# A conditioned sequence model on one Trainium2 core: the second layer as one stage

## The reference, cut to what matters

```python
xn = layernorm(x, norm_scale, norm_bias)
q, k, v = xn @ Wq + bq, xn @ Wk + bk, xn @ Wv + bv
k = where(mask, -inf, k);  v = where(mask, 0.0, v)
q = softmax(q over the 32 features of a head)
k = softmax(k over the 1024 rows of a batch)
attn = einsum('bhse,bhsd->bhed', k, v)          # 32 x 32 for each head
y = einsum('bhtd,bhed->bhte', q, attn)
h = silu(layernorm(y) * (1 + scale(emb)) + shift(emb))
out = x + h @ film_out_W + film_out_b
```

## Time and profile before

| | us |
|---|---|
| device time, median of 3 runs | 6635.8 (6633.12 to 6639.58) |
| span of the profiled execution | 6635.1 |
| p2, from its first ScalarE table load to the first load of the next stage | 1722.7 to 2093.4: 370.7 |
| linear_attention | 2093.4 to 2326.5: 233.1 |
| p3, to the first table load of ssm_inputs | 2326.5 to 2492.95: 166.5 |

### The profile page before, as it was taken

How to read it: one execution, slowest core, us unless ns; L and a number is a source line. 1 busy time by engine, 2 the same in 40 slices (tenths; PEclk the granted TensorE clock), 3 DMA queues, 4 the chain that set the end, 5 groups by cost and what they waited for, 6 DMA issues and landing times. The chain is left out here.

```text
span 6635.1 us, 86376 instructions
## 1 busy us (share of the span) xinstructions
PE 5586.8 (84%) x30592; PEld 3543.3 (53%) x30592; DVE 4664.3 (70%) x5664; ACT 4230.4 (64%) x6243; POOL 2482.7 (37%) x1098
## 2 busy tenths in 40 slices
PE   6999999997897578999578888887999578888884
PEld 2446666664443543444466666663444366666662
DVE  2329999995322544554799999994554599999993
ACT  1218888884111424554798998982555599999992
POOL 0000000000000000000599999991000299999995
PEclk9999999998998789999799999999999799999997
DMA  5344424323323343333555565552333555655554
GB/s 202 146 134 95 96 65 100 76 56 115 138 99 117 138 165 121 142 144 148 164 152 156 160 161 158 157 141 104 142 143 130 163 160 155 158 152 154 154 151 171
DMA packets 598091, 909.84 MB, mean 137 GB/s; under 512 B 104473, under 2 KB 243865, under 8 KB 597157
## 3 DMA queue, kind: packets, MB, share of 16 engines
q1 hardware_dynamic: 586212, 879.10, 44.4%
q0 software_dynamic: 5120, 16.78, 0.7%
q10 hardware_dynamic: 6336, 8.52, 0.4%
HBM read 577.82 MB, written 326.39 MB: 136 GB/s over the span
## 5 line engine op out<-in xcount | busy, mean ns | idle before, releaser
L1624 POOL TENSOR_TENSOR scan_hC<-scan_h,scan_Crep 128x1024 f32<-128x1024 f32 x1024 | 2395.0, 2371 | 2619.5 <-DVE scan_h L1857 2594.7
L1788 ACT ACTIVATE scan_a<-scan_dt,scan_A 128x512 f32<-128x512 f32 x2048 | 1368.9, 697 | 94.0 <-DVE scan_h L1857 76.7
L1658 PE MATMUL scan_y<-ident,scan_hC 128*128 128x128 f32 x8192 | 1112.0, 279 | 294.8 <-POOL scan_hC L1624 289.9
L1658 PEld LDWEIGHTS scan_y<-ident,scan_hC 128*128 128x128 f32 x8192 | 902.2, 141 | 682.4 <-POOL scan_hC L1624 634.5
L1857 DVE TENSOR_TENSOR_SCAN scan_h<-scan_a,scan_carry,scan_h 128x512 f32<-128x512 f32 x1024 | 1216.8, 1260 | 17.9 <-ACT scan_a L1788 14.9
L1857 DVE TENSOR_TENSOR_SCAN scan_h<-scan_a,scan_h 128x512 f32<-128x512 f32 x1024 | 1155.5, 1200 | 59.2 <-ACT scan_a L1788 58.5
L1764 ACT COPY scan_h<-scan_drive 128x1024 f32<-128x1024 f32 x1024 | 1042.2, 1018 | 164.6 <-PE scan_drive L1646 152.5
L1646 PE MATMUL scan_drive<-scan_Bd,scan_dT 128*128 128x256 f32 x4096 | 749.7, 305 | 130.0 <-ACT scan_h L1764 79.0
L1646 PEld LDWEIGHTS scan_drive<-scan_Bd,scan_dT 128*128 128x128 f32 x4096 | 557.7, 192 | 183.3 <-issue 96.3
L791 DVE CUSTOM_DVE_ANT_0 att_sm<-att_S,att_mneg 128x1024 f32<-128x1024 f32 x512 | 622.1, 1215 | 15.0 <-POOL att_mneg L717 14.8
L849 ACT ACTIVATE att_pr<-att_sm,att_nmax 128x1024 f32<-128x1024 f32 x512 | 590.5, 1153 | 56.3 <-DVE att_nmax L791 44.0
(11 more groups left out here) (162 smaller groups left out, 5967.4 us busy)
## 6 DMA issues: line engine op xcount, KB each, us to landing
scan_dT<-scratch_dtuT SPq DMA_DIRECT2D x512, 256.0 KB, 5.5
scratch_dtuT<-ssmin_dT SPq DMA_DIRECT2D x128, 512.0 KB, 3.5
scan_Crep<-scratch_bc SPq DMA_DIRECT2D x64, 1024.0 KB, 9.1
att_q<-scratch_q_split SPq DMA_DIRECT2D x256, 128.0 KB, 4.3
att_k<-scratch_k_split SPq DMA_DIRECT2D x256, 128.0 KB, 4.5
scratch_uD<-ssmin_uD SPq DMA_DIRECT2D x64, 512.0 KB, 3.4
scratch_z<-ssmin_zt SPq DMA_DIRECT2D x128, 256.0 KB, 2.1
scratch_dt<-ssmin_dt SPq DMA_DIRECT2D x64, 512.0 KB, 2.6
```

Source lines behind the costliest of these rows:

```text
L1624: nc.gpsimd.tensor_tensor(hC[k % 2][:], of, Crep[:, 2 * p:2 * p + 2, :], ALU.mult).then_inc(s["scaled"].handle, 1)
L1658: last = nc.tensor.matmul(y[j][:, t, :], hC[k % 2][:, i, t * P:(t + 1) * P], ident[:], start=(p == 0 and i == 0 and t == 0), stop=False, i ...
L1788: nc.scalar.activation(a[(2 * k + i) % 3][:], dt[j][:], ACT.Exp, scale=A[:, m, 2 * p + i:2 * p + i + 1]).then_inc(s["decayed"].handle, 1)
```

## The change

`project` p2, `linear_attention` and `project` p3 become one stage, `linear_layer`, written out without a loop. k, q, v and y stay in SBUF; only x1 is read (once for the statistics, once as the residual) and x2 written. One TensorE order runs through all batches (`order` in the diff): k of this batch, the transposes ("w") and the products ("o") of the film projection of the batch before, q, v, the transposes of k and q, attn ("a"), the transposes ("x") of the next batch's x, and y. Each entry takes the next of the 8 banks and waits until the entry 8 back has been emptied. x and xT have one buffer each instead of two; y lies in q's buffer; the softmax of q runs in two halves of 2048 columns; y is now copied by VectorE; residual and result have 4 tiles each instead of 8. In `Rows`, arguments were added so that the source of the rows may be tiles already in SBUF (`made`) and xT may have one buffer (`turned=1`).

```diff
-        project(core, "p2", ...)
-        linear_attention(core, ident, io, scr)
-        project(core, "p3", ...)
+        linear_layer(core, ident, eps, io, cols, scr)

+        def order():
+            yield from (("x", 0, k) for k in range(8))
+            for it in range(B):
+                yield from (("k", it, k) for k in range(8))
+                if it:
+                    yield from ((kind, it - 1, k) for kind in ("w", "o") for k in range(8))
+                yield from ((kind, it, k) for kind in ("q", "v", "kt", "qt") for k in range(8))
+                yield "a", it, 0
+                if it + 1 < B:
+                    yield from (("x", it + 1, k) for k in range(8))
+                yield from (("y", it, k) for k in range(8))
+            yield from ((kind, B - 1, k) for kind in ("w", "o") for k in range(8))
...
+            # SyncE, after the first x, the tables, the 4 weights, rows and mask
+            for it in range(B):
+                if it + 1 < B:
+                    xs.load(sp, it + 1)      # waits until x(it) has been transposed
+                    load_mask(it + 1)        # waits until mneg(it) is made
+                if it:
+                    leave(it - 1)            # 4 residual loads ahead, then store a tile, load a tile
+            leave(B - 1)
...
+            # TensorE, for each entry e of order()
+                if e >= 8:
+                    before, of, which = entries[e - 8]
+                    pe.wait_ge(taken[before].handle, taken[before].at(per[before] * of + which + 1))
+            # kt waits for k_norm; qt for q_norm of its half; a for all of kt and v taken;
+            # y for a taken and its half of qt; o for its half of w; k for its half of x
...
+            # ScalarE
+            for it in range(B):
+                for k in range(8):
+                    take_k(it, k)
+                    if k == 1 and it:
+                        ys.root(act, it - 1)
+                    if k == 5:
+                        exp_k(it, 0)
+                exp_k(it, 1)
+                if it:
+                    for k in range(8):
+                        ys.take(act, it - 1, k, *at_bank("w", it - 1, k))
+                exp_k(it, 2)
+                exp_k(it, 3)
+                if it + 1 < B:
+                    xs.root(act, it + 1)
+                for h in range(2):
+                    exp_q(it, h)
+                for t in range(TT):
+                    take_kt(it, t)
+                for k in range(8):
+                    take_qt(it, k)
+                for k in range(8) if it + 1 < B else ():
+                    xs.take(act, it + 1, k, *at_bank("x", it + 1, k))
+            ys.root(act, B - 1)
+            for k in range(8):
+                ys.take(act, B - 1, k, *at_bank("w", B - 1, k))
...
+            # VectorE
+            for it in range(B):
+                make_mneg(it)
+                if it:
+                    stats(ys, it - 1)
+                shift_k(it, 0)
+                if it:
+                    ys.center(dve, it - 1)
+                for m in range(1, KT):
+                    shift_k(it, m)
+                for t in range(TT):
+                    if it:
+                        take_o(it - 1, t)
+                    if it + 1 < B:
+                        xs.take_stats(dve, it + 1, t)
+                    if t == 3:
+                        norm_k(it)
+                if it + 1 < B:
+                    xs.aggregate(dve, it + 1)
+                for t in range(TT):
+                    take_q(it, t)
+                    if t == 1 and it + 1 < B:
+                        xs.center(dve, it + 1)
+                    if t == 3:
+                        shift_q(it, 0)
+                shift_q(it, 1)
+                for t in range(TT):
+                    take_v(it, t)
+                    if t == 1:
+                        norm_q(it, 0)
+                    if t == 3:
+                        norm_q(it, 1)
+                take_a(it)
+                for t in range(TT):
+                    take_y(it, t)
+            stats(ys, B - 1)
+            ys.center(dve, B - 1)
+            for t in range(TT):
+                take_o(B - 1, t)
```

More of the change, by code:

```diff
@@ L404, in stage_added @@
         n = len(self.x)
-        for k in range(2 * n):
+        for k in range(2 * n) if self.made is None else ():
             self.rows_in[k].stage_added(self.per_half * B // n)
@@ new lines, in linear_layer @@
+        row = [sb(f"row{n}", [P, D]) for n in range(3)]
+        kp = sb("keep", [P, B, TT])
+        res, out = ([sb(f"{n}{k}", [P, D]) for k in range(4)] for n in ("res", "out"))
+        banks = [psum(f"bank{k}", [P, HALF]) for k in range(8)]
+        kinds = ("k", "q", "v", "kt", "qt", "a", "y", "o")
+        per = {**{kind: 8 for kind in kinds}, "a": 1, "x": 8, "w": 8}
+        taken = {kind: core.count("lin_taken_" + kind) for kind in kinds}
+        xs = Rows(core, sb, 1, scr["x1"], scr["tab"][2], ACT.Identity, eps, ident, turned=1)
@@ new lines, in linear_layer @@
+        ys = Rows(core, sb, 1, None, scr["tab"][3], ACT.Silu, eps, ident, turned=1, made=(y, taken["y"]))
+        taken["x"], taken["w"] = xs.evacuated, ys.evacuated
+        lin = {n: core.count("lin_" + n) for n in ("mask_in", "k_shift", "k_exp", "k_norm", "q_max", "q_shift", "q_exp",
+                                                   "q_norm", "q_sums", "k_inverse", "mneg", "cleared")}
+        w = lambda eng, n, value: eng.wait_ge(lin[n].handle, lin[n].at(value))
+        full, stored, res_in = core.bank_full, core.stage_stored, core.slot_in
@@ new lines, in linear_layer @@
+        weights_in = [core.count(f"weights_in{n}") for n in range(4)]
+        N_CONST = 16 * 4
+        def order():
[10 more added lines that the diff above has]
+            yield from ((kind, B - 1, k) for kind in ("w", "o") for k in range(8))
@@ new lines, in linear_layer, with await_full @@
+        entries = list(order())
+        place = {entry: e for e, entry in enumerate(entries)}
+        at_bank = lambda *entry: (banks[place[entry] % 8], full[place[entry] % 8], place[entry] // 8 + 1)
+        def await_full(eng, *entry):
+            _, c, uses = at_bank(*entry)
+            eng.wait_ge(c.handle, c.at(uses))
+        qv = lambda h: q[:, 4 * h:4 * h + 4, :].rearrange("p k (g e) -> p (k g) e", e=DH)
+        some = lambda x, h: x[:, 4 * H * h:4 * H * (h + 1)]
+        wide = lambda x, h: some(x, h).unsqueeze(2).broadcast_to([P, 4 * H, DH])
@@ L915, in store_y @@
[L915 to L930, removed]
@@ new lines, in leave @@
+            def leave(it):
+                for t in range(4):
+                    load_res(it, t)
+                for t in range(TT):
+                    store_out(it, t)
+                    if t + 4 < TT:
+                        load_res(it, t + 4)
+            xs.load(sp, 0)
+            xs.load_table(sp)
+            load_weight(0, "Wk")
+            load_mask(0)
+            load_weight(1, "Wq")
+            load_row(0, 2)
+            load_weight(2, "Wv")
+            load_row(1, 3)
```

323 lines of the change are left out of this document (200 added, 123 removed).

## The result

The changed kernel takes 6475.36 us, median of 4 runs (6471.62 to 6479.7), beside 6637.69 for the kernel before in the same comparison: ratio 0.9753, 95% interval 0.9739 to 0.9767. The forecast was 6467 (6452 to 6498). The span of the profiled execution is 6469.7 us, 165.4 less than before. In the table further down two of e8's six executions (6611.58 and 21171.61 us, at a granted clock of 0.92 and 0.52) were disturbed: its median of 6461.37 holds them, that of the other four is 6457.4, its ratio is formed without them, and of the single executions of e4 and e5 it can't be told.

The account below looks back on a forecast made before the run. TensorE bounds p2; in linear_attention no engine does, they wait in turn. Start, products, transposes, attn and y, waits and tail sum to 601.1 us for 770.25, 169.2 less: 6467 us, range 6452 to 6498.

Parts of the forecast that it names:

- One TensorE list that sets the pace: New stage: priced as one TensorE list, TensorE busy over 93% at a clock of 0.97 or more.
- Start, 20.9: Start of the stage: first x load, statistics and 8 transpose groups before products, 20.9 us, as in ssm_inputs.
- Products, 439.5: 128 products in the stage, 32 for each batch, 3.43 us each: 439.5 us.
- Transposes 49.7, attn and y 59.3: TensorE's small work: 14 blocks of 8 transpose groups, 49.7 us; eight attn and y groups of 7.41, 59.3 us.
- w to o, 9.0: Film transposes to film products: TensorE waits 3.0 us for ScalarE's chain, three times, 9.0 us.
- Tail, 21.4: After the last y: uncovered chain 15.1 us, slow-clock product start 2.1, end 4.2; together 21.4 us.
- VectorE, ScalarE, SyncE hidden: Whole stage: these engines' work fits beside TensorE's; VectorE 80 us a batch against TensorE's 142.
- Slack of 1.6 us at the v tiles: Last v tile emptied at 56.4, its bank wanted by a transpose group at 58.0: VectorE may be 1.6 us late.
- rival (2): VectorE late at the v tiles by 5 to 8 us each batch: 20 to 32 us, 6486 to 6498; chance 0.13.
- Rival (1), the clock falls in the small work: Transposes at 1.2 GHz cost 54 us, total 6520; attn and y too, 6580; chance 0.07.
- Rival (3), 745 us without overlap: Interleaving does not overlap anything: four batches of 181 us plus 21, stage 745, total 6611; chance 0.03.
- The stage's sum, 601.1: All terms of the TensorE list added: 601.1 us for the new stage, against 770.25 before.

Follow-up runs that it names:

- e8: Changed kernel with film transposes between the last k products; last batch: y statistics tile by tile during ScalarE's copies, attn between q's transpose halves; stage 581.64 us, median 6461.37.
- e4: Changed kernel with two unused reductions of half of q (4.6 us) on VectorE before the last four v tiles of each batch; stage 600.56 us.
- e5: Changed kernel with four unused reductions of half of q (9.2 us expected) on VectorE before the last four v tiles of each batch; stage 622.67 us.
- e2: Changed kernel without interleaving: each batch in the order of its own dependences, one stage, nothing through DRAM; stage 717.35 us, median 6594.54.
- e3: Changed kernel with 32 MB read and 32 MB written more in the stage, unused, on GpSimd's queue; stage 600.51 us, median 6472.82.
- e6: Changed kernel with ScalarE's second exponential of k moved behind the evacuations of the film transposes; stage 593.62 us, median 6475.83.

## Why the prediction was right, point by point

- *One TensorE list that sets the pace.* Right: 561.6 of 600.6 us busy, 93.5%, at 0.97 of the clock, and e2, busy 585.2 of 717.4 us (82%) with the same 2048 records, shows that this comes from the order.
- *Start, 20.9.* Right: 1725.98 to 1746.75, 20.8; ssm_inputs was the same form.
- *Products, 439.5.* The pace was right; that they could start at the low clock behind w stood only among the rivals, as "2.1 for each of three, 6 us". It was 1.8 for two of three, 3.5 us.
- *Transposes 49.7, attn and y 59.3.* Slightly large: a block takes 3.49, 48.9 for 14 (and 14 times 8 times 0.44 is 49.3, not 49.7); attn and y take 7.14 each from start to start, 57.1. Rows 3 gave 7.41 as the length of a group, which holds the last matmul's own end.
- *w to o, 9.0.* 2.61 three times, 7.8. The chain was right: 6.3 us from the last k product to the first film product (1881.39 to 1887.66), for 6.5.
- *Tail, 21.4.* It was 20.6, by two misses of opposite sign. From the last y's end to the first product 15.1 was forecast (its terms add up to 15.0) and it was 16.4 (2278.49 to 2294.93). The wait itself was right, 10.1; but from the first transpose to the first product I took 4.6 from the start of p3, where the products begin behind four groups of transposes. In the new order all eight stand in front, and at the lower clock they took 6.3. In return the products behind them ran at the full clock (27.63), and the 2.1 for a slow start did not come. The end took 4.1, for 4.2.
- *VectorE, ScalarE, SyncE hidden.* Right: outside the start, the waits before o and the tail, TensorE's timeline has no idle time. e3 and e4 show it for the traffic and VectorE. The half-width passes took 2.29 us, the nearly proportional value.
- *Slack of 1.6 us at the v tiles* and with it rival (2), "a lateness of 5 to 8 us gives 20 to 32 us": wrong by its working, as e4 shows. The chance of 0.13 that hung on it was too large.
- *Rival (1), the clock falls in the small work.* Refuted by the window over k's and q's transposes (1.00 through 6.95 us). The Trainium skill ("TensorE: Matmul & The Clock Gate", Part 4: PE-mode transpose) says that the clock's high level does not engage for transposes. This window and e6 against after (same transposes, shorter idle time, no fall) decide against it here.
- *Rival (3), 745 us without overlap.* The mechanism was run as e2 and gave 717. I had counted each chain in full, with 17.15 in front of k's transposes as in rows 3; e2 makes v before k and q behind it, and there has no idle time in front of k's transposes.
- *The stage's sum, 601.1 for 600.55.* The mechanism is shown; that the sum is right to 0.6 is in part luck. The clock behind w cost 3.5 that the sum did not have, and against it stand 0.8 too much for the transposes, 2.2 for attn and y, about 1 for the wait before o and 0.8 for the tail.
- *The total.* 6475 for 6467: the profiled execution's span was 3.8 longer than forecast, 0.6 less in the stage and 4.3 more in the rest, which was longer than in the one of before, within the 20 us over which it spreads. The step from this span to the median of device times was 5.7, where I had 0.7: the same execution's device time was 1.9 over its span, and 3.7 under the median. The repetitions gave 6468 to 6470.

## What to carry to other kernels

Where three stages each show an engine idle for another reason, write the engine with the most work as one list over all batches and put every chain of the other engines beside products of another batch: here that was worth 117 us over a stage without any interleaving, such a stage in SBUF 53 over the three before, which were interleaved in part, and the 64 MB of traffic, added again beside the finished list, cost nothing. Then look at the few places that are left uncovered, a switch of ScalarE's table at a hand-over and the tail, and hold work back for them: 24 us more. Ask of a delay not how far the next use is, but how much waiting lies between the delayed instructions.

## What was not expected of the hardware

The granted clock held through single waits of 1.33 us (in front of the last y) and 1.48 us (e6), and fell in 15 of 21 batches after 2.6 us, each fall costing 1.6 to 1.8 us of products. In e5 it fell in four of four batches behind a wait of 1.82 us and some shorter ones. Identical instructions outside the stage took between 5861.8 and 5881.7 us from one profiled execution to another, while the TensorE-bound stage repeated within 1.0 us.
